# Attention operands kept as pairs of 16-bit floats, scaled by bounds that the chip computes

## What is computed

```python
h = layernorm(x) * (1 + ca) + sa                      # [2048, 512]
q, k, v = (einsum('bpm,hmd->bphd', h, W) + b for each of Q, K, V)   # 16 heads of 128
logits = where(causal, q @ k.T / sqrt(128), -1e5)
x = x + ga * (einsum(softmax(logits) @ v, O_w) + O_b)
h = layernorm(x) * (1 + cb) + sb
# router: softmax, top 4 of 64 experts; experts and two shared experts of width 512
x = x + gb * (routed(h) + shared(h))
```

## Time and profile before

| | us |
|---|---|
| median of 3 runs (2079.01 to 2082.61) | 2079.69 |
| the profiled execution, its own time | 2079.52 |
| its span from first to last instruction | 2077.7 |
| PE busy | 1998.1 (96%) |
| DVE busy | 1386.0 (67%) |
| ACT busy | 1105.7 (53%) |
| POOL busy | 380.5 (18%) |
| mean granted TensorE clock | 0.989 |

### The profile page before, as it was taken

How to read it: one execution, slowest core, us unless ns; L and a number is a source line. 1 busy time by engine, 2 the same in 40 slices (tenths; PEclk the granted TensorE clock), 3 DMA queues, 4 the chain that set the end, 5 groups by cost and what they waited for, 6 DMA issues and landing times.

```text
span 2077.7 us, 33132 instructions
## 1 busy us (share of the span) xinstructions
PE 1998.1 (96%) x9863; PEld 1500.9 (72%) x9865; DVE 1386.0 (67%) x3219; ACT 1105.7 (53%) x1638; POOL 380.5 (18%) x393
## 2 busy tenths in 40 slices
PE   6799999999999999999999999789999999999988
PEld 3677777777777777777777777567887778777766
DVE  7687787787687687786786876647555943333376
ACT  4476676676676585675675766433334134444311
POOL 5210010110110110110110110534000122222264
PEclk9999999999999999999999999899999999999999
DMA  6399798798888888888988987895422088999665
GB/s 218 61 180 173 150 181 169 151 181 170 155 176 170 166 165 170 165 168 165 175 167 158 183 171 149 171 215 171 137 83 66 0 269 287 312 300 317 212 194 178
DMA packets 932174, 366.07 MB, mean 176 GB/s; under 512 B 754800, under 2 KB 885920, under 8 KB 932128
## 3 DMA queue, kind: packets, MB, share of 16 engines
q1 hardware_dynamic: 921888, 331.93, 71.1%
q0 software_dynamic: 10240, 33.56, 5.2%
HBM read 138.86 MB, written 41.94 MB: 87 GB/s over the span
## 4 chain that ended last, share of the span: by engine, by line
PE 81%; DMA 6%; POOL 4%; SPq 4%; DVE 3%; issue 2%; ACT 1%; DVEq 0%; POOLq 0%; ACTq 0%
PE gen L1575 12%; PE gen L1577 11%; PE gen L1576 11%; PE strip L1575 7%; PE strip L1576 7%; PE strip L1577 7%; PE pv L1575 6%; PE pv L1576 6%; PE pv L1577 6%; PE strip L1871 5%; SPq L472 3%; PE strip L1878 2%; DMA wd_sb<-in_L_ffn_Wd 2%; DMA gath<-yb_dram,slot_u 2%; POOL gath L811 2%
## 5 line engine op out<-in xcount | busy, mean ns | idle before, releaser
L1182 DVE SCALAR_TENSOR_TENSOR p_lo<-exps,rinv,p_hi 128x512 f16<-128x512 f32 (+3 forms) x256 | 391.4, 1555 | 36.2 <-ACT p_hi L864 35.7
L855 ACT ACTIVATE exps<-exps,nbias 128x128 f32<-128x128 f32 (+15 forms) x256 | 306.9, 1199 | 142.6 <-DVE nbias L1168 142.6
L864 ACT ACTIVATE p_hi<-exps,rinv 128x512 f16<-128x512 f32 (+3 forms) x256 | 334.7, 1353 | 31.5 <-DMA pT<-p_lo 14.5
L1158 DVE TENSOR_SCALAR_CACHE_REDUCE exps<-strip 128x512 f32<-128x512 f32 x384 | 249.3, 686 | 137.0 <-PE strip L1577 134.8
L1575 PE MATMUL strip<-kT_hi,qT_hi 128*128 128x512 f32 (+3 forms) x640 | 237.1, 370 | 14.3 <-DVE kT_lo L1130 8.0
L1576 PE MATMUL strip<-kT_lo,qT_hi 128*128 128x512 f32 (+3 forms) x640 | 234.7, 367 | 0.0
L1577 PE MATMUL strip<-kT_hi,qT_lo 128*128 128x512 f32 (+3 forms) x640 | 234.6, 367 | 0.0
L1575 PE MATMUL pv<-pT,v 128*128 128x512 f16 (+3 forms) x640 | 223.5, 349 | 5.7 <-DMA pT<-p_lo 5.7
L1576 PE MATMUL pv<-pT,v 128*128 128x512 f16 (+3 forms) x640 | 222.7, 348 | 0.0
L1577 PE MATMUL pv<-pT,v 128*128 128x512 f16 (+3 forms) x640 | 219.6, 348 | 0.0
L711 POOL TENSOR_TENSOR wq_lo<-wq_raw,wq_hi 128x512 fp32r<-128x512 f32 x16 | 20.7, 1296 | 1073.1 <-ACT wq_hi L834 1073.1
(11 more groups left out here) (236 smaller groups left out, 4348.1 us busy)
## 6 DMA issues: line engine op xcount, KB each, us to landing
at_dram<-at_f SPq DMA_DIRECT2D x64, 256.0 KB, 2.6
wg_sb<-in_L_ffn_Wg SPq DMA_DIRECT2D x64, 256.0 KB, 4.7
wu_sb<-in_L_ffn_Wu SPq DMA_DIRECT2D x64, 256.0 KB, 5.1
wd_sb<-in_L_ffn_Wd SPq DMA_DIRECT2D x64, 256.0 KB, 5.9
yb_dram<-yb SPq DMA_DIRECT2D x64, 256.0 KB, 5.7
a_f<-at_dram SPq DMA_DIRECT2D x58, 256.0 KB, 2.8
pT<-p_hi SPq DMA_TRANSPOSE x320, 3.4
pT<-p_lo SPq DMA_TRANSPOSE x320, 3.3
```

The lines of the kernel that those rows point to most:

```text
L855: nc.scalar.activation(row, row, ACT.Exp, bias=nbias[:, t:t + 1], accum_out=rsum[:, t:t + 1]).then_inc(row_probs, 1)
L864: nc.scalar.activation(p_hi16[:, 0:j + 1, t, :], row, ACT.Copy, scale=rinv[:, t:t + 1]).then_inc(p_hi, 1)
L1158: nc.vector.tensor_scalar(exps[:, t, 512 * ch:512 * ch + w], strip[u % STRIPS][:, 0:w], SCALE, None, ALU.mult, ALU.max, accum_out=cmax[:, ...
L1182: nc.vector.scalar_tensor_tensor(p_lo16[:, 0:j + 1, t, :], row, rinv[:, t:t + 1], p_hi16[:, 0:j + 1, t, :], ALU.mult, ALU.subtract).then_i ...
```

## The change

Input, weights of the projections, queries and keys become pairs of `F16`, 2 bytes a value. So that they fit the range of that type, they are scaled by factors which the chip works out from bounds: per input feature (`h_bound`, from the modulation), per column of a head's weights (`fac`, in `factors`) and per head (`qk_sum`, from which `logit_now` is made; the exponential takes it as its scale and `nbias` is multiplied by it). The value scale is part of `fac` now, so `value_bound` and `value_scale` go.

For each head POOL's `split_lo` and `value_weight_sizes` are replaced by `prepare`: three multiplications by feature as soon as the weights have landed, a sum of sizes, and after `factors` three times multiply, cast, subtract. ACT's three copies at the start of stage 3 go, and three `Abs` come in stage 1 between the high halves of the keys and of the values (`weight_sizes`). PE gets one matmul of 384 columns in stage 2 (`weight_bounds`). DVE gets `factors` after the keys of stage 2, `factor_columns` in stage 3 ahead of the third `probs_lo`, and the low half of the values of stage 3 moves behind the second `score_row`. SP loads the weights at the top of the loop, ahead of stage 1. The clearing of `exps` before the first score is three strided pieces in place of one. The output weights `wo` lie in a buffer of their own shape over the same memory. And the gathers of the end have two semaphores a buffer in place of four: POOL waits, ahead of every second gather, until both gathers of the pair before have landed, and DVE waits for a pair.

```diff
-        hT_hi = a.place("hT_hi", [P, DC, S], F32R)
-        hT_lo = a.place("hT_lo", [P, DC, S], F32R)
+        hT_hi = a.place("hT_hi", [P, DC, S], F16)
+        hT_lo = a.place("hT_lo", [P, DC, S], F16)
...
-        w_hi_t = [a.place(f"w{n}_hi", [P, DC, P], F32R) for n in "qkv"]
+        w_hi_t = [a.place(f"w{n}_hi", [P, DC, P], F16) for n in "qkv"]
...
-        kT_hi = a.place("kT_hi", [P, S], F32R)
-        qT_hi = a.place("qT_hi", [P, 512], F32R)
+        kT_hi = a.place("kT_hi", [P, S], F16)
+        qT_hi = a.place("qT_hi", [P, 512], F16)
...
-                if j == 1:
-                    load_weights(h)
...
             with sp.Fori(0, H - 1) as h:
+                load_weights(h)
...
+            def by_feature(n):
+                return nc.gpsimd.tensor_tensor(raw[n][:], raw[n][:], h_bound[:].unsqueeze(2).to_broadcast([P, DC, P]),
+                                               ALU.mult)
...
+            def split(n, h):
+
+                wait_alone(fac_ready, h + 1)
+                nc.gpsimd.tensor_tensor(raw[n][:], raw[n][:], fac[:, n:n + 1, :].to_broadcast([P, DC, P]), ALU.mult
+                                        ).then_inc(w_step, 1)
+                wait_alone(w_step, h * 6 + (2 * n + 1))
+                nc.gpsimd.tensor_copy(w_hi_t[n][:], raw[n][:]).then_inc(w_step, 1)
+                wait_alone(w_step, h * 6 + (2 * n + 2))
+                nc.gpsimd.tensor_tensor(w_lo_t[n][:], raw[n][:], w_hi_t[n][:], ALU.subtract).then_inc(w_split, 1)
...
+            pool.wait_ge(ln_turned, NT)
+            clear_above(0)
+            clear_above(1)
             ln_lo(3)
-
             pool.wait_ge(ln_split, NT)
-            nc.gpsimd.memset(exps[:], 0.0).then_inc(exps_clear, 1)
+            clear_above(2)
...
-                    n = t * TOPK + k - GATHERS_OUT
-                    if n >= 0:
-                        pool.wait_ge(g_landed[n // TOPK % GATHS][n % TOPK], 16 * (n // (TOPK * GATHS) + 1))
+                    n = 2 * t + k // 2 - 1
+                    if k % 2 == 0 and n >= 0:
+                        pool.wait_ge(g_landed[n // 2 % GATHS][n % 2], 32 * (n // (2 * GATHS) + 1))
...
+            def weight_sizes(h):
+
+                act.wait_ge(w_summed, h)
+                for n in range(3):
+                    act.wait_ge(w_featured, h * 3 + (n + 1))
+                    ins = nc.scalar.activation(w_abs[:, n], raw[n][:], ACT.Abs)
+                ins.then_inc(abs_ready, 1)
...
-                    for kind in "qkv":
-                        gen_hi_of(kind, nxt[1], nxt[0])
+                    gen_hi_of("q", nxt[1], nxt[0])
+                    gen_hi_of("k", nxt[1], nxt[0])
+                    if j == 1 and weights:
+                        weight_sizes(h + 1)
+                    gen_hi_of("v", nxt[1], nxt[0])
...
+            def factors(h, src):
+
+                wait_alone(w_bounds, h + 1)
+                nc.vector.tensor_scalar(bound[:], src, 1.0 / W_TOP, 1e-15, ALU.mult, ALU.add).then_inc(bound_out, 1)
+                wait_alone(bound_out, h + 1)
+                wait_alone(w_split, h * 3)
+                nc.vector.tensor_tensor(fac_tmp[:, 0, :], bound[:, 0, :], bound[:, 1, :], ALU.mult).then_inc(fac_step, 1)
+                for n in (0, 2):
+                    nc.vector.reciprocal(fac[:, n, :], bound[:, n, :])
+                wait_alone(fac_step, h * 5 + 1)
+                nc.vector.tensor_reduce(qk_sum[:], fac_tmp[:, 0, :], AX_X, ALU.add).then_inc(fac_step, 1)
+                wait_alone(fac_step, h * 5 + 2)
+                nc.vector.reciprocal(qk_inv[:], qk_sum[:]).then_inc(fac_step, 1)
...
+            def factor_columns(h):
+
+                wait_alone(fac_ready, h + 1)
+                nc.vector.tensor_tensor(fac_tmp[:], fac[:], ident[:].unsqueeze(1).to_broadcast([P, 3, P]), ALU.mult
+                                        ).then_inc(fac_step, 1)
...
+                if j == QB - 1:
+                    gen_out_of("v", QB - 1, h)
...
+                    if j == 2 and weights:
+                        factors(h + 1, bounds)
-                    if jn != 1:
+                    if jn in (0, 2):
                         gen_out_of("v", jn, hn)
```

More of the change, by code:

```diff
@@ L736, in _ @@
-            split_lo(2, 0)
+            pool.wait_ge(h_bounded, 1)
+            pool.wait_ge(abs_ready, 1)
+            for n in range(3):
+                by_feature(n).then_inc(w_featured, 1)
+            pool.wait_ge(w_featured, 3)
+            split(0, 0)
             ln_lo(0)
+            split(1, 0)
             ln_scales(0, 2)
@@ L854, in exp_row @@
                 row = exps[:, t, 0:(TB * j + t + 1) * P]
-                nc.scalar.activation(row, row, ACT.Exp, bias=nbias[:, t:t + 1],
+                nc.scalar.activation(row, row, ACT.Exp, bias=nbias[:, t:t + 1], scale=logit_now[:, 0:1],
                                      accum_out=rsum[:, t:t + 1]).then_inc(row_probs, 1)
@@ L931, in _ @@
             for hh, j, prev, nxt in stages(H - 1, True)[0:2]:
-                stage(hh, j, prev, nxt)
+                stage(hh, j, prev, nxt, weights=False)
             def take_a(u):
@@ L1183, in probs_lo, with stage @@
                                                ALU.mult, ALU.subtract).then_inc(p_lo, 1)
[L1185 removed]
+            def stage(h, j, nxt, weights=True):
                 score_row(h, j, 0)
@@ L1220, in ln_stat_of @@
                 ln_stat(0, b, x_sb)
+            bounds = strip[STRIPS - 1][:, 0:3 * P].rearrange("p (n d) -> p n d", n=3)
             def normalise_x(b):
@@ L1277, in _ @@
             for hh, j, prev, nxt in stages(H - 1, True)[0:2]:
-                stage(hh, j, nxt)
+                stage(hh, j, nxt, weights=False)
             def ln2_lo(b, ch):
@@ L1609, in project, with weight_bounds, score @@
                 last.then_inc(gen_done, 1)
-            def value_bound(h, o):
-                pe.wait_ge(abs_ready, h + 1)
-                for ch in range(DC):
-                    last = nc.tensor.matmul(o, wv_abs[:, ch, :], h_most_bf[:, ch:ch + 1], start=ch == 0,
-                                            stop=ch == DC - 1)
-                last.then_inc(v_bound, 1)
-            def score(h, j):
+            def weight_bounds(h, o):
+                pe.wait_ge(w_summed, h + 1)
+                nc.tensor.matmul(o[:, 0:3 * P], ones_w[:], w_sum[:].rearrange("p n d -> p (n d)"), start=True, stop=True
+                                 ).then_inc(w_bounds, 1)
+            def score(h, j, weights=True):
                 pe.wait_ge(gen_out, nth("k", j, h) + GENS)
@@ L1622, in score @@
                     u = strips_before(j) + n
+                    if j == QB - 1 and n == STRIPS - 1 and weights:
+                        pe.wait_ge(bound_out, h + 2)
                     pe.wait_ge(strip_out, h * NSTRIP + (u + 1))
@@ L1652, in ln2_turn, with stage @@
                 last.then_inc(ln_turned, 1)
-            def stage(h, j, prev, nxt):
-                score(h, j)
+            def stage(h, j, prev, nxt, weights=True):
+                score(h, j, weights)
                 if j == 0:
@@ L1682, in _ @@
             ln_turn(0)
+            pe.wait_ge(h_bounded, 1)
+            pe.wait_ge(abs_ready, 1)
+            for ch in range(DC):
+                nc.tensor.matmul(gen[2][:, 0:3 * P].rearrange("p (n d) -> p n d", n=3), h_rows[:, ch, :],
+                                 w_abs[:, :, ch, :], start=ch == 0, stop=False)
+            pe.wait_ge(w_summed, 1)
+            nc.tensor.matmul(gen[2][:, 0:3 * P], ones_w[:], w_sum[:].rearrange("p n d -> p (n d)"), start=False,
+                             stop=True).then_inc(w_bounds, 1)
             ln_turn(1)
```

248 lines of the change are left out of this document (147 added, 101 removed).

## The result

| | before | changed |
|---|---|---|
| median, us | 2079.35 | 2187.74 |
| lowest and highest of 4 runs | 2076.69 to 2082.61 | 2183.19 to 2189.09 |
| span of the profiled execution | 2077.7 | 2185.8 |
| PE busy | 1998.1 | 1957.9 |
| DVE busy | 1386.0 | 1473.3 |

The change makes the kernel slower: the ratio is 1.0517, with a 95% interval of 1.0495 to 1.0538. The forecast was 2163 with a range of 2112 to 2212. The measured time lies above the 2145 to 2180 that the forecast called likeliest for itself, and within the wide range. PE is busy 40 us less, and the kernel takes 108 us more.

What follows compares the result with a forecast made beforehand. PE was taken as the bound in stage 0, PE with DVE closely behind in stages 1 to 3, POOL's gathers (or PE with them) at the end. 2079.5 + 19 (heads) + 63 (gather pairs) + 1.5 (start) = 2163 us, range 2112 to 2212.

Steps and rivals of the forecast that it cites:

- rival 2: In the heads: contention is worse, DVE's `p_lo` meets POOL also in stage 3; heads +58 us, 2202 in all; chance 0.17.
- The pairs: Gathers at the end: POOL waits for each whole pair, 5.2 to 5.6 us a pair; +63 us, upper end +75.
- The heads: Head loop: low keys of stage 0 come 3.1 us late, so each head is 1.3 longer; +19 us over 15 heads.
- a reserve of 1.3: End of a head: DVE finishes stage 0's low keys 1.3 us before PE's first score of the next head needs them.
- The meeting of POOL and `p_lo`: Stage 1: POOL's three products by feature slow DVE's `p_lo` by 2.15 us a head, 1.2 of it reaching stage 2.
- the prediction's second estimate: Stage 1, by the Trainium skill's contention rule: `p_lo` waits up to 1.3 us per POOL product, 3.9 a head, time 2189.
- The start: Before the first score: clearing `exps` in three strided pieces behind POOL's weight splits delays it 1.5 us (-3 to +6).
- That PE stays the bound: All four stages of the heads: PE remains the bound and gives 70 us back, 2074 in all, faster; chance 0.05.
- the 4.6 that I counted for PE: PE's gain a head from 16-bit operands: 2.3 us on 228 matmuls of 512 columns, as much again estimated for the rest.
- Rival 3: Gathers at the end: a pair's landings take 2.0 us or less, period 3.9, only +20, about 2120 in all; chance 0.08.
- rival 5: PE's matmuls: the types don't change their pitch, stage 0's 0.5 us goes, 7 us added, 2170; within the likeliest case.
- Rival 1: In the heads: DVE keeps its reserve, meetings fall into gaps, reciprocals are cheap; heads gain 18 us, 2126 in all; chance 0.20.

## Why the prediction was right, step by step

The sum was 2079.5 + 19 + 63 + 1.5 = 2163. Measured in the same terms it is 108 rather than 83.5. The two large terms were the right ones, and each was too small. That 2188 lies inside the range is in part luck: the room for slower heads came from more meetings with POOL, in stage 3 too (rival 2), and from dearer reciprocals. But `p_lo` of stage 3 met nothing (2.33 and 2.35, as alone) and the reciprocals cost what was taken, while the heads lost their time in waits that the sum didn't have.

- **The pairs (+63, measured +77).** Mechanism shown from both sides, size too small: I took the shortest landings, "since the short landings are the commoner ones", and 5.2 us a pair. It was 5.7, 31 times 0.5 more. In the mean of the 31 pairs the second gather starts 1.45 behind the first (taken: 1.25), lands 3.69 later (3.3), and 0.56 goes by until the next pair (0.65). In no pair did the first gather land last. The upper end that I gave, +75, would have been the right one to take.
- **The heads (+1.3 each over 15, measured +2.0 over 14, and -0.5 in head 0: +19 against +28).** PE's saving in stage 0 was 0.80, not 0.5. The costs of `factors` (3.4, measured 3.66), of a long reciprocal (0.9; two took 1.67), of `factor_columns` (1.6, measured 1.87) were right in size, and the run without the reciprocals showed that they count in full. But the way to the time was not the one forecast. I let all delays run down DVE's chain to the low keys of the next head's stage 0, 3.1 late against a reserve of 1.3. PE does wait there, but only 0.49. It had already waited 1.97 at stage 2 and 2.15 in stage 3 for the strips behind `factors`.
- **The meeting of POOL and `p_lo` (2.15, measured 1.30 and 1.58).** From the start of the first `p_lo` to the low queries it took 5.45 before and 6.75 and 7.03 in two heads. In the head shown the three meetings cost 0.36, 0.52 and 0.44, each less than the 1.0 of the earlier trace rows, and together far less than the 3.9 of the prediction's second estimate. Here a step failed in its way. I let 1.2 of it arrive at the first strip of stage 2 on DVE. It arrived at PE, which stood 1.97 for the low keys of stage 2: I had read the reserve of `kT_lo` in stage 0 and not the one in stage 2, where two rows of the kernel before leave 0.25 (the low keys end at 499.32, PE's first score starts at 499.57):

```profile
498.58 0.74 DVE L1130 SCALAR_TENSOR_TENSOR kT_lo<-gen,bias_now,kT_hi 128x512 fp32r<-128x512 f32 x1
...
499.57 0.39 PE L1575 MATMUL strip<-kT_hi,qT_hi 128*128 128x512 f32 x1
```

- **The clock was not in the sum.** A PE that had no wait before in the loop now has one of 2 us, and in 6 of 14 heads that cost 1.1 us behind it, 6.4 us in all. The term stood at nothing, without a reason.
- **The start (+1.5, measured +4.1).** The clearing ends late, at 71.54, but what the first score (73.34) waits for longest is DVE's work on `gb_bc`, which ends at 73.02. This is late, as far as the rows tell, because PE waits 9.31 us for the first low halves `hT_lo`, at 42.15: POOL multiplies the first weights, waits for their factors and splits them ahead of `hT_lo`. No run tests it.

```profile
42.15 0.58 PE L1682 MATMUL gen<-hT_hi,wq_hi 128*128 128x512 f16 x1 [9.31 <-POOL hT_lo L737]
```

- **The rivals.** That PE stays the bound (my case for a faster kernel) is out even without the factors: the types alone give 2.0 us of the 4.6 that I counted for PE. Rival 3 (short landings) is out by the 5.7 a pair, and rival 5 (no gain from the types) by the 0.8 of stage 0. Rival 1 is out because DVE lost its reserve, and the meeting of rival 2 didn't come.

## What to carry to other kernels

A wait that holds all of a transfer group before the next is issued costs a full landing per group; keep one group more in flight, or wait for single transfers. Before an engine off the critical path gets new work, read its reserve at every place where the bound engine waits for it, not only at one, and place the new work in the largest idle stretch. Then look at what that idle stretch was hiding: here it was the jump of a loop.

## What the runs showed that I had not expected

The same wait of 2.11 us on PE is followed by 1.2 GHz for some 3 us in 4 of 14 heads and by the full clock in the others. A loop's jump on DVE costs 1.1 us a pass once little idling is left to hide it, and the trace puts it down to the engine whose strip comes next. It left DVE's sequencer without an instruction for 3.5 us in the change and for 0.3 in the kernel before. POOL suffers from the meeting as well: the product of 128x384 took 1.68 beside `p_lo` and 0.83 where it ran without it.
